# Feature look-up of a graph attention layer: fp32 node features against three bf16 parts

## The reference, cut to what matters

```
h     = (x @ W.T).reshape(n, 8, 32)
alpha = einsum(h[src], a_src) + einsum(h[dst], a_dst)
enc   = relu(edge_attr @ edge_W.T + edge_b).reshape(-1, 8, 32)
alpha = alpha + sum(enc * h[dst], axis=-1)
alpha = where(alpha >= 0, alpha, 0.2 * alpha)
attn  = exp(alpha - segment_max(alpha, dst)[dst]) / segment_sum(exp(...))[dst]
out   = segment_sum(h[src] * attn, dst) + bias
```

## Time and profile before

| | us |
|---|---|
| median of 3 runs | 5015.8 (5006.75 to 5021.97) |
| profiled execution, its own time | 5025.15 |
| its span, first to last instruction | 5023.4 |
| TensorE products busy | 3385.1 (67%) |
| TensorE weight loads busy | 2324.6 (46%) |
| VectorE, ScalarE, GpSimd busy | 1969.7, 1211.3, 2043.2 |
| mean granted clock of TensorE | 0.784 |

### The profile page before, as it was taken

How to read it: one execution, slowest core, us unless ns; L and a number is a source line. 1 busy time by engine, 2 the same in 40 slices (tenths; PEclk the granted TensorE clock), 3 DMA queues, 4 the chain that set the end, 5 groups by cost and what they waited for, 6 DMA issues and landing times. The chain is left out here.

```text
span 5023.4 us, 50647 instructions
## 1 busy us (share of the span) xinstructions
PE 3385.1 (67%) x14657; PEld 2324.6 (46%) x14657; DVE 1969.7 (39%) x5074; ACT 1211.3 (24%) x3052; POOL 2043.2 (41%) x2054
## 2 busy tenths in 40 slices
PE   3878762397888883211787783425993985798796
PEld 2666651284544442200564552212561663347686
DVE  5545565215666668500797123000005435102101
ACT  3444430032222221100785111000011212103232
POOL 4666637403555557577001542773006433000021
PEclk8676675698988886555898897656996997898798
DMA  4444420004776661200663332102413214342112
GB/s 155 160 161 155 162 101 14 0 1 146 210 200 194 185 195 57 77 10 19 197 242 132 101 99 86 61 13 72 151 59 128 64 63 142 118 153 86 38 37 74
DMA packets 278409, 542.54 MB, mean 108 GB/s; under 512 B 61218, under 2 KB 187110, under 8 KB 277508
## 3 DMA queue, kind: packets, MB, share of 16 engines
q1 hardware_dynamic: 199876, 396.17, 23.5%
q0 software_dynamic: 78272, 143.18, 10.6%
HBM read 370.70 MB, written 168.47 MB: 107 GB/s over the span
## 5 line engine op out<-in xcount | busy, mean ns | idle before, releaser
L1172 PE MATMUL bank<-layer_gnn_h_nodes,layer_gnn_s_onehot_t 128*128 x1664 | 554.3, 462 | 96.2 <-issue 58.8
L1124 POOL DMA_INDIRECT layer_gnn_s_rows<-gat_rows,src_cols x416 | 401.7, 966 | 366.9 <-DMA kept_rows<-layer_gnn_s_rows 208.1
L1421 PE MATMUL bank<-layer_gnn_w_onehot,layer_gnn_w_part 128*128 128x128 f32 x1664 | 308.8, 317 | 333.3 <-issue 247.8
L143 POOL DMA_INDIRECT edge_weights<-shares,share_cell x416 | 461.3, 1109 | 128.4 <-issue 128.4
L2522 PE MATMUL bank<-layer_gnn_b_weights,xn_nodes 128*128 128x400 f32 x768 | 319.0, 555 | 286.4 <-issue 216.7
L495 POOL DMA_INDIRECT layer_gnn_sum_rows<-xn_rows,src_cols x416 | 424.6, 1021 | 199.4 <-issue 102.2
L133 POOL DMA_INDIRECT edge_counts<-repeats,count_cell x416 | 423.9, 1019 | 126.4 <-issue 126.4
L1421 PEld LDWEIGHTS bank<-layer_gnn_w_onehot,layer_gnn_w_part 128*128 128x128 f32 x1664 | 237.8, 208 | 404.6 <-issue 269.1
L554 PE MATMUL bank<-layer_gnn_sum_onehot,layer_gnn_sum_rows 128*128 128x128 f32 x1664 | 363.9, 381 | 80.5 <-issue 55.3
L1172 PEld LDWEIGHTS bank<-layer_gnn_h_nodes,layer_gnn_s_onehot_t 128*128 128x128 f32 x1664 | 320.5, 214 | 195.0 <-issue 119.8
L554 PEld LDWEIGHTS bank<-layer_gnn_sum_onehot,layer_gnn_sum_rows 128*128 128x128 f32 x1664 | 315.2, 277 | 132.0 <-issue 89.5
(11 more groups left out here) (599 smaller groups left out, 5672.1 us busy)
## 6 DMA issues: line engine op xcount, KB each, us to landing
kept_rows<-layer_gnn_s_rows SPq DMA_DIRECT2D x104, 512.0 KB
layer_gnn_w_rows<-kept_rows SPq DMA_DIRECT2D x104, 512.0 KB
edge_weights<-layer_gnn_sum_zeros SPq DMA_DIRECT2D x56, 800.0 KB
layer_gnn_b_weights<-edge_weights SPq DMA_DIRECT2D x56, 800.0 KB
layer_gnn_gcn_sum_counts<-edge_counts SPq DMA_DIRECT2D x50, 896.0 KB
layer_gnn_s_dst_across<-in_dst_row SPq DMA_DIRECT2D x104, 256.0 KB
edge_counts<-layer_gnn_w_no_edges SPq DMA_DIRECT2D x25, 896.0 KB
layer_ffn_e_w<-in_l1f_w SPq DMA_DIRECT2D x16, 1024.0 KB
```

The costliest lines, as they stand in the source:

```text
L143: nc.gpsimd.indirect_dma_start(g.weights, bass.IndirectOffsetOnAxis(ap=g.share_cell[:, t:t + 1].bitcast(U32), axis=0), g.shares[:, t:t + 1 ...
L1124: nc.gpsimd.indirect_dma_start(rows[:, t % U, :], None, htable, bass.IndirectOffsetOnAxis(ap=g.srcc[:, t:t + 1].bitcast(U32), axis=0)).the ...
L1172: last = nc.tensor.matmul(g.ps[4 + t % 4][:, 0:D + HEADS], onehot_t[:, t % 4, k, :], hflat[:, ds(w * AW + (k * AW + HEADS), D + HEADS)], s ...
L1421: last = nc.tensor.matmul(g.ps[t % 4][:, c * P:(c + 1) * P], part[:, t % 4, c * P:(c + 1) * P], onehot[:, t % 4, :], start=True, stop=True)
```

## The change

`hs` becomes a ring of 8 tiles instead of 26, and is kept in fp32 only until its store has landed: an eviction from the ninth tile on waits for the store of the tile that lay in its slot; the stores count on two semaphores in turn. From each evicted tile three bf16 parts are made of columns 8 to 272: ScalarE rounds the features to the high part, VectorE subtracts it, ScalarE rounds the rest to the middle part, VectorE subtracts that and writes the low part. The first part lies in the storage of the normed rows, the others in a new tile. In the edge scores the one-hot is written in bf16, and the look-up of each node tile is three bf16 products in place of one in fp32.

```diff
-        hs, w_rows = sb("h_nodes", [P, NT, AW]), sb("edge_w_rows", [ENC, D], BF16)
+        w_rows, later_parts = sb("edge_w_rows", [ENC, D], BF16), sb("h_parts", [P, 2, NT, LW], BF16)
+        first_part = g.xn[:, :, :]....bitcast(BF16)[:, 0:NT * LW].rearrange("p (t n) -> p t n", t=NT)
+        hparts = [first_part, later_parts[:, 0, :, :], later_parts[:, 1, :, :]]
...
+            hs, h_rest = sb2("h_nodes", [P, 8, AW]), sb2("h_rest", [P, 4, LW])
...
-                    sp.dma_start(by_tile[:, lo:hi, :], hs[:, lo:hi, 0:HEADS + D]).then_inc(rows_stored, 16)
+                    sp.dma_start(by_tile[:, lo:hi, :], hs[:, lo % 8:lo % 8 + hi - lo, 0:HEADS + D]).then_inc(rows_stored[k % 2], 16)
...
+                def cut(t):
+                    if t < NT:
+                        act.wait_ge(evicted, t + 1)
+                        nc.scalar.activation(hparts[0][:, t, :], hs[:, t % 8, HEADS:AW], ACT.Copy).then_inc(high, 1)
+                    if t >= 1:
+                        act.wait_ge(rested, t)
+                        nc.scalar.activation(hparts[1][:, t - 1, :], h_rest[:, (t - 1) % 4, :], ACT.Copy).then_inc(middle, 1)
                 for t in range(EARLY, NT):
                     take(t)
+                    if t >= EARLY + 2:
+                        cut(t - EARLY - 2)
+                for t in range(NT - EARLY - 2, NT + 1):
+                    cut(t)
...
                 def evict(t):
                     dve.wait_ge(product, t + 1)
-                    nc.vector.tensor_copy(hs[:, t, :], g.ps[2 + t % 3][:, 0:AW]).then_inc(evicted, 1)
+                    if t >= 8:
+                        dve.wait_ge(rows_stored[t // 4 % 2], 16 * (t // 8))
+                    nc.vector.tensor_copy(hs[:, t % 8, :], g.ps[2 + t % 3][:, 0:AW]).then_inc(evicted, 1)
+                def leave(t):
+                    dve.wait_ge(high, t + 1)
+                    if t >= 4:
+                        dve.wait_ge(low, t - 3)
+                    nc.vector.tensor_tensor(h_rest[:, t % 4, :], hs[:, t % 8, HEADS:AW], hparts[0][:, t, :], ALU.subtract).then_inc(rested, 1)
+                def lowest(t):
+                    dve.wait_ge(middle, t + 1)
+                    nc.vector.tensor_tensor(hparts[2][:, t, :], h_rest[:, t % 4, :], hparts[1][:, t, :], ALU.subtract).then_inc(low, 1)
...
                 for t in range(NT):
                     evict(t)
+                    if t >= 4:
+                        leave(t - 4)
+                    if t >= 6:
+                        lowest(t - 6)
...
-        dst, onehot_t = sb("dst_across", [P, PARTS, Q * P], I32), sb("onehot_t", [P, 4, 2, P])
+        dst, onehot_t = sb("dst_across", [P, PARTS, Q * P], I32), sb("onehot_t", [P, 4, 2, P], BF16)
...
                 for k in range(2):
-                    last = nc.tensor.matmul(g.ps[4 + t % 4][:, 0:D + HEADS], onehot_t[:, t % 4, k, :],
-                                            hflat[:, ds(w * AW + (k * AW + HEADS), D + HEADS)], start=(k == 0), stop=(k == 1))
+                    for j in range(3):
+                        last = nc.tensor.matmul(g.ps[4 + t % 4][:, 0:LW], onehot_t[:, t % 4, k, :],
+                                                flat[j][:, ds(w * LW + k * LW, LW)], start=(k == 0 and j == 0), stop=(k == 1 and j == 2))
                 last.then_inc(looked, 1)
```

More of the change, by code:

```diff
@@ L887 @@
 AW = HEADS + D + HEADS
+LW = D + HEADS
 def layer1_gnn(nc, g, a, table):
@@ L909, in gat_features @@
         sb = lambda n, s, d=F32: stack.enter_context(nc.sbuf_tensor(g.tag + n, s, d))
-        hs, w_rows = sb("h_nodes", [P, NT, AW]), sb("edge_w_rows", [ENC, D], BF16)
+        w_rows, later_parts = sb("edge_w_rows", [ENC, D], BF16), sb("h_parts", [P, 2, NT, LW], BF16)
+        first_part = g.xn[:, :, :].rearrange("p t d -> p (t d)").bitcast(BF16)[:, 0:NT * LW].rearrange("p (t n) -> p t n", t=NT)
+        hparts = [first_part, later_parts[:, 0, :, :], later_parts[:, 1, :, :]]
         ids = g.acc[:, :, :].rearrange("p t d -> p (t d)")[:, CE + 2:CE + 2 + 2 * ET].rearrange("p (t k) -> p t k", k=2)
@@ L914, in gat_features @@
             sb2 = lambda n, s, d=F32: s2.enter_context(nc.sbuf_tensor(g.tag + "f_" + n, s, d))
-            loaded, edge_w_in, attr_in, w_stored, w_placed, parts_stored, rows_stored = (sem(n) for n in (
-                "loaded", "edge_w_in", "attr_in", "w_parts_stored", "w_rows_placed", "parts_stored", "rows_stored"))
+            loaded, edge_w_in, attr_in, w_stored, w_placed, parts_stored, *rows_stored = (sem(n) for n in (
+                "loaded", "edge_w_in", "attr_in", "w_parts_stored", "w_rows_placed", "parts_stored", "rows_stored0", "rows_stored1"))
             stat, aggr, root, inv, shifted, by_dve, by_act = (sem(n) for n in ("stat", "aggr", "root", "inv", "shifted", "normed_dve", "normed_act"))
@@ L924, in gat_features @@
             attr, rest, split = sb2("attr", [P, n]), sb2("rest", [P, n]), sb2("split", [P, 3, n], BF16)
+            hs, h_rest = sb2("h_nodes", [P, 8, AW]), sb2("h_rest", [P, 4, LW])
+            high, rested, middle, low = sem("h_high"), sem("h_rested"), sem("h_middle"), sem("h_low")
             edge_w, w_rest, w_split = sb2("edge_w", [4, D]), sb2("w_rest", [4, D]), sb2("w_split", [4, 3, D], BF16)
@@ L955, in _ @@
                 sp.wait_ge(parts_stored, 32)
-                sp.wait_ge(rows_stored, 16 * len(STORES))
+                for k in range(2):
+                    sp.wait_ge(rows_stored[k], 16 * ((len(STORES) + 1 - k) // 2))
             @block.gpsimd
@@ L1096, in _, with edge_scores @@
                                                 ALU.mult, ALU.add).then_inc(listed, 1)
+                for t in range(NT - 4, NT):
+                    lowest(t - 2)
+                    leave(t)
+                for t in range(NT - 2, NT):
+                    lowest(t)
                 dve.wait_ge(listed, 2)
-        edge_scores(nc, g, hs, a, parts, w_rows, htable, kept, alpha, dst_chunks, ids)
-def edge_scores(nc, g, hs, a, attr_parts, w_rows, htable, kept, alpha, dst_chunks, ids):
+                dve.wait_ge(low, NT)
+        edge_scores(nc, g, hparts, a, parts, w_rows, htable, kept, alpha, dst_chunks, ids)
+def edge_scores(nc, g, hparts, a, attr_parts, w_rows, htable, kept, alpha, dst_chunks, ids):
     with ExitStack() as stack:
@@ L1116, in edge_scores @@
         block = stack.enter_context(nc.Block(g.tag + "edge_scores"))
-        hflat = hs[:, :, :].rearrange("p t d -> p (t d)")
+        flat = [v.rearrange("p t n -> p (t n)") for v in hparts]
         @block.gpsimd
```

## The result

The changed kernel takes 5068.1 us (median of 4, 5063.7 to 5082.6), the kernel before beside it 5011.3 (4994.9 to 5022.0). The ratio is 1.0121, 95% interval 1.0086 to 1.0157, so 57 us more, between 43 and 79. Forecast were 5052 us, 36 more than the 5015.8 shown. The two executions that were profiled differ by 44 us.

The account below looks back on a forecast made before the run. It took TensorE's notices, late during GpSimd's gathers and limited by the count of loads and products, as the bound. Edge scores +23 and front +10 made 33 us: 5058 against the profiled execution, 5052 as median; range 4925 to 5185.

Parts of the forecast that it names:

- The front: Preparation of node tiles before the edge scores: added conversions, subtractions and store waits cost +10 us, from +3 to +20.
- TensorE's pace: Edge scores: an undisturbed tile takes 1.05 us (0.98 to 1.14) against 1.30.
- a call's sequencer work: Edge-score look-up: register operation and issue bound each product call from above by 0.14 us; six take 0.67 to 0.83 us.
- Late notices: Edge scores: while GpSimd issues gathers, notices of TensorE's instructions get out at a limited rate; 185 us go where pace breaks.
- the 104 us of TensorE: Edge scores: 0.25 us less a tile over 416 tiles, on TensorE alone at full clock.
- The clock: TensorE's granted clock, 0.85 in a typical edge-score stretch, would be under 0.85 after the change.
- The count: Edge scores: number of loads and products, 10 to 14 a tile, limits the notices; stage 749 us, 23 more; chance 0.60.
- reckoning of one run: Edge scores: twelve gathers, 50 instructions ahead, then 2.4 per us; twelve tiles go from 22.5 to 23.3 us.
- mix of runs: Edge scores: 0.77 long runs of 12 gathers and 0.23 short of 4 give 1.746 us a tile, changed 1.80.
- rival C: Edge scores: GpSimd and DMA queues set the mean, stage stays 726 us, only the front is paid; 5026 us, chance 0.12.
- Rival B: Edge scores: TensorE's time counts, late notices stay as they are; 4922 to 5005 us, value 4960, chance 0.20.

Follow-up runs that it names:

- six products without registers: Changed kernel with a constant place in the parts for all tiles, so no register operation ahead of its six products; 1.0015 against the kernel before, stage 731 us.
- one part: Changed kernel with only the first of the three bf16 parts in the look-up, two products a tile; 1.0001 against the kernel before, stage 718 us.
- run at 812 us: Changed kernel as it is, run again on a chip where the kernel before takes 5053 us; 1.0158, stage 812 us.
- before with eight ahead: Kernel before, each score-stage gather waiting until the tile eight before it has been used; 4979 us against 5053, ratio 0.9850, stage 666 us.
- before with rows by SP: Kernel before, score-stage source rows loaded by SP as plain DMAs of the same size instead of GpSimd's gathers; 1.0174, stage 624 us.
- two parts: Changed kernel with the first two of the three bf16 parts in the look-up, four products a tile; 1.0048 against the kernel before, stage 739 us.

## Why the prediction was right, and which step of it failed

The direction and the total were right: 57 us were lost where 36 were forecast. In part that is luck. The front held, but of the stage's 52 us only 23 were forecast, and those by a rule that the runs refute.

**The front** was forecast at +10 and cost 8.5 to 9 us, by the terms named: VectorE works through 78 steps 0.34 us apart, the ninth eviction waits.

**TensorE's pace** was taken as 1.05 us a tile and is 0.99. The top of my range for a call's sequencer work, 0.14 us, was too high; the bottom, the products' own length, was it.

**Late notices** were rightly seen as what breaks the pace, as beginning in runs of gathers and ending with GpSimd's stop, and as keeping the 104 us of TensorE from being seen. The traces hold it directly, as they record a semaphore's increments, by which one engine tells another that it is through, with their times. In the score stage of the kernel before, 131 of the 300 recorded increments of line 1165 come over 0.1 us after the last product of that line that had ended, at worst 5.6 us; those at 1504.55 and 1509.50 are the ones that start ScalarE at 1504.57 and 1509.52. In that trace ScalarE's and VectorE's own increments are never over 0.01 us late. The clock followed as forecast (0.86 to 0.77 in the stage).

**The count** is the step that failed: "What counts is how many loads and products there are". With 6, 8 fewer than changed and 4 fewer than before, the stage stayed at 718 us; with 10 in bf16 it was 739; with 14 and no register operation 731; with 10 in fp32 727 to 730. The six products without registers, as many as changed, lose nothing against the kernel before. My reckoning of one run (50 run ahead, 2.4 per us after) reached +23 us by a rule that the runs refute. Its mix of runs, 0.77 long and 0.23 short, was fitted to the measured 1.746 us and not read: 56 runs of 4 are 224 of the 416 tiles, and runs of 12 or more hold 88. As far as the runs tell, the loss of the stage goes with the register operations (832 in all: 727 and, with one part, 718 us; 1664: 739; 2496: 779 and, on another chip, 812; none beside six products: 731), which I had left out of the sum with the words "with the register operations counted it would be worse". Worse it was: 52 where I took 23.

What the runs show in its place: the breaks do not follow the number of loads and products, they go with GpSimd's running ahead (eight tiles in place of sixteen: 666 us, on the one slow chip where that ran). The stage is 520 us of issuing gathers and what GpSimd waits for kept rows, which is 188 to 225 us on the slow chips for any look-up from 2 to 6 products, and 257 and 288 for the changed kernel as it is. For the lighter look-ups that is nearest to rival C, to which I gave 0.12: GpSimd and its ring set the mean and only the front is paid. For the change itself C was wrong too, as the stage grew by 52 us; and it named the DMA queues' load as the reason, which the chip at 3985 us with its share of 0.92 refutes. Rival B, that the 104 us come off, is what happened on that other chip, cut to about 17 by GpSimd's 1.25 us a gather (an estimate: 8.7 us gained by the whole and 8.5 paid in the front; the kernel before has no trace there).

**Open.** Why TensorE's notices come late on the slow chips and not on the chip at 3985 us, while the same gathers are issued at the same 1.25 us, isn't settled; no run changed that alone. The late operations of TensorE's sequencer (55 register, semaphore and move operations of over 0.5 us in the changed kernel, none in the kernel before, none on the chip at 3985 us) go with the loss of 48 us. But one part has 116 of them and loses nothing, and the run at 812 us has 40, so they are not shown to be its cause.

The recording itself is the rival that stays. The traces miss increments where the notices are late:

| score stage (416 products of the attributes) | increments recorded | over 0.1 us late | at worst, us |
|---|---|---|---|
| before, slow chip | 300 | 131 | 5.6 |
| changed, slow chip | 355 | 204 | 5.2 |
| one part, slow chip | 277 | 131 | 7.3 |
| before with eight ahead, slow chip | 295 | 154 | 2.4 |
| changed, chip at 3985 | 414 | 0 | 0.01 |
| before with rows by SP, chip at 3989 | 416 | 0 | 0.01 |

(Late means: after the last product of that line that had ended, so the true delay can be longer.) On the slow chips nearly half of VectorE's and ScalarE's increments are missing too, 173 of 416 of line 1201 in the kernel before. In the same trace at 2420 to 2650 us, without gathers, TensorE's 290 are all there and none is late. So on the slow chips records are lost just where gathers run and notices come late, which fits a recording that can't keep up there. It doesn't prove it. The Trainium skill ("NOTIFIC — the notification-queue block", 7.1, Overflow) says that the block through which engines report their instructions holds them back inside rather than lose a record, so that reporting can throttle an engine. That would look like these breaks and could differ between chips. A limit on TensorE's records alone is refuted by the version with one part. No run here was made without a recording, so no run shows it, and how much of the loss an unrecorded execution would have stays open as well.

## What to carry to other kernels

Where two engines and a ring run at nearly one pace (here 1.30, 1.25 and 1.07 us a tile), write down for each of them its work and its waits before making one faster. Here GpSimd's 520 us of gathers were a floor known ahead, so no look-up could win more than 207 of the 727 us. What it waits for kept rows was not known ahead: it was 188 to 288 us on the slow chips (without the bound of eight tiles) and nothing on the other, since it depends on how late VectorE is. Where an engine's running ahead holds the others up, a bound on how far it may run can be worth more than the edit of the engine that looks busiest: 74 us won by one wait here, against 57 lost on the first chip by six cheaper products and 82 on the same chip. And run the kernel before beside each version on the same chip, as the sign of a change of 1% turned here from one chip to another.

## What the runs showed of the hardware

- One program took 5011 to 5053 us on some chips and 3985 to 3989 on another, a fifth less, with the same gather pace and the same undisturbed tile; what differed is the time between a product and those who wait for it: in the changed kernel the increments of line 1204 come up to 5.2 us late on the first chip and never over 0.01 us on the other. A profile of one chip can hide which engine is the bound on the next.
- With one part TensorE's granted clock was 0.50 for the whole stage and with two parts 0.56, where six products had 0.77 and fp32 0.86. Cheaper products left gaps (TensorE busy 391 of 718 us with one part), and the clock fell to 1.2 GHz; the stage was 718 us all the same.
- A load of register values (the window numbers, line 1160) held TensorE's sequencer for 2.6 us in the middle, thirteen times in the kernel before, twelve of them in the stage; the row gives ns min/median/max:

```profile
L1160 PEldq TENSOR_LOAD <-dst_window x13: 2128/2595/2881, 1191.5 to 1869.1; - x13
```
